# Layer-0 experts of a two-layer transformer kernel: VectorE takes both halves of the router-weight multiply, GpSimd takes the rotary add of the next step

## The reference, cut to what matters

```python
xn = _layernorm(x, axis=-1)
x = x + _L0_attn_ref(xn, ...) + _L0_ffn_ref(xn, ...)

# in _L0_attn_ref: the same projection serves as queries and keys, and both are rotated
bq = bq * jnp.cos(qf) * qs + _rotate_half(bq) * jnp.sin(qf) * qs
bk = bk * jnp.cos(freqs) * inv_s + _rotate_half(bk) * jnp.sin(freqs) * inv_s
sim = jnp.einsum('bwie,bwje->bwij', bq, bk)
attn = jax.nn.softmax(sim, axis=-1)
out = jnp.einsum('bwij,bwje->bwie', attn, bv)
return out @ w_out.T

# in _L0_ffn_ref: one shared expert and eight routed ones, weighted per token (top 2)
h1 = jax.nn.gelu(jnp.einsum('td,edh->teh', flat, rw1) + rb1[None], approximate=False)
expert_out = jnp.einsum('teh,ehd->ted', h1, rw2) + rb2[None]
mixed = jnp.einsum('ted,te->td', expert_out, weights)
return (shared_out + mixed)
```

## Time and profile before

| what | value |
|---|---|
| median of 3 runs | 1160.11 us (1159.56 to 1161.54) |
| the profiled execution's own time | 1158.52 us |
| its span in the trace | 1157.2 us |
| mean granted clock of TensorE | 0.964 of full speed |
| busy: PE, DVE, ACT, POOL | 90%, 62%, 45%, 40% of the span |
| stages `experts0` of steps 2 to 6 in the trace | about 40 us each, one every 133 us |

### The profile page before, as it was taken

One profiled execution on the slowest core, in us unless ns is written; L12 is line 12 of the kernel. 1 busy time (PEld: TensorE's weight loads), 2 busy tenths in 40 slices (PEclk: granted clock), 3 DMA queues, 4 the chain that ended last, 5 costly groups with the idle time before them and its releaser, 6 DMA issues.

```text
span 1157.2 us, 13293 instructions
## 1 busy us (share of the span) xinstructions
PE 1045.4 (90%) x4472; PEld 634.5 (55%) x4472; DVE 713.7 (62%) x1485; ACT 519.4 (45%) x1209; POOL 457.7 (40%) x337
## 2 busy tenths in 40 slices
PE   4877856899999998999999998999989999989998
PEld 2543434546655565656655565655655466655655
DVE  4845525564884758574884848665784848712743
ACT  3442453326264443735255453645356363634322
POOL 4229310274215642084413742075411852043434
PEclk9898877989999999999999999999999999989999
DMA  6041000322023220233004220232104220232151
GB/s 239 1 138 37 9 1 1 113 73 72 11 73 87 64 55 10 90 78 82 18 14 128 64 73 0 84 80 78 37 10 122 64 73 1 83 76 73 37 119 47
DMA packets 34581, 72.77 MB, mean 63 GB/s; under 512 B 4553, under 2 KB 5330, under 8 KB 34130
## 3 DMA queue, kind: packets, MB, share of 16 engines
q1 hardware_dynamic: 33074, 68.59, 21.0%
q10 hardware_dynamic: 1440, 3.35, 0.8%
HBM read 69.04 MB, written 2.88 MB: 62 GB/s over the span
## 4 chain that ended last, share of the span: by engine, by line
PE 65%; DVE 9%; issue 7%; POOL 4%; ACT 2%; DMA 0%; DVEq 0%; POOLq 0%; ACTq 0%
PE ps L689 9%; PE ps L577 7%; PE ps L440 6%; PE ps L441 6%; PE ps L442 6%; PE ps L512 5%; PE ps L488 4%; PE ps L500 4%; PE ps L664 3%; POOL pw L1742 2%; PE ps L585 2%; PE ps L635 2%; PE ps L471 2%; PE ps L653 1%; PE ps L643 1%
## 5 line engine op out<-in xcount | busy, mean ns | idle before, releaser
L1742 POOL TENSOR_TENSOR pw<-pw,wb 128x512 f32<-128x512 f32 x64 | 94.9, 1483 | 215.7 <-ACT pw L1002 190.8
L577 PE MATMUL ps<-pw,w_w 128*128 128x512 f32 x288 | 146.3, 618 | 24.0 <-POOL pw L1742 24.0
L1078 ACT ACTIVATE wide<-ps 128x512 f32<-128x512 f32 x136 | 80.9, 595 | 177.3 <-PE ps L442 176.5
L1749 POOL TENSOR_TENSOR atc<-atc,wide 128x512 f32<-128x512 f32 x64 | 82.4, 1289 | 168.1 <-DVE atc L1470 168.1
L1002 ACT ACTIVATE pw<-ps,w_cols 128x512 f32<-128x512 f32 x144 | 99.0, 687 | 107.8 <-PE ps L442 104.6
L1355 DVE TENSOR_TENSOR pw<-pw,wb 128x512 f32<-128x512 f32 x64 | 62.3, 974 | 128.5 <-ACT pw L1002 121.5
L961 ACT ACTIVATE pw<-ps,nmax 128x256 f32<-128x256 f32 x256 | 117.2, 473 | 25.7 <-DVE nmax L1291 25.6
L1291 DVE TENSOR_REDUCE nmax<-ps 128x4 f32<-128x1024 f32 x64 | 78.2, 1224 | 58.7 <-PE ps L488 58.2
L512 PE MATMUL ps<-pt,vr 128*64 128x256 f32 x512 | 74.7, 416 | 27.6 <-DVE pt L1300 27.5
L1300 DVE COPY pt<-ps 128x512 f32<-128x512 f32 x128 | 82.3, 685 | 23.7 <-PE ps L500 23.6
L577 PEld LDWEIGHTS ps<-pw,w_w 128*128 128x128 f32 x288 | 51.8, 193 | 79.4 <-POOL pw L1742 47.2
(11 more groups left out here) (219 smaller groups left out, 2188.4 us busy)
## 6 DMA issues: line engine op xcount, KB each, us to landing
wb<-scratch SPq DMA_DIRECT2D x128, 256.0 KB, 4.0
wb<-scratch SPq DMA_DIRECT2D x32, 512.0 KB, 5.5
wide<-scratch SPq DMA_DIRECT2D x16, 512.0 KB, 6.1
xin<-in_x SPq DMA_DIRECT2D x8, 256.0 KB, 2.7
out<-wide SPq DMA_DIRECT2D x8, 256.0 KB, 2.1
w_w<-in_w ACTq DMA_DIRECT2D x1, 1152.0 KB, 11.0
wb<-in_w SPq DMA_DIRECT2D x1, 1152.0 KB, 11.2
w_ed<-in_ed ACTq DMA_DIRECT2D x1, 1024.0 KB, 15.8
```

The costliest lines, as they stand in the source:

```text
L577: pe.matmul(bank(ACC), w2[:, e, c, :], hid[:, n % 4, :], start=n == 0, stop=n == 2 * E0 + 1).then_inc(*DOWN0.one)
L1742: pool.tensor_tensor(hid[:, n % 4, :], hid[:, n % 4, :], wb[:, e, :], ALU.mult).then_inc(*HID_POOL.one)
L1749: pool.tensor_tensor(hh[h], hh[h], sgl[:, (c + 1) % 3, :], ALU.mult).then_inc(*HH_POOL.one)
```

## The change

DVE's `hidden` now multiplies both halves of each expert, and POOL's is gone. POOL's `rope_add` takes the place of DVE's in the stages `experts0` (those that DVE does for step 0, ahead of and in `attention(0)`, stay). POOL's stage is written anew: per pair of heads it is `normalise`, `rope_turn`, `rope_add`; in step 0 it is two `split_staged`, `rope_turn`, `rope_add`, and the four `normalise` come at the end. The two events of `hidden` become one, `HID`, with 16 counts per step.

```diff
@@ events
-        HID_DVE, HID_POOL = event("hid_dve", E0), event("hid_pool", E0)
+        HID = event("hid", 2 * E0)
@@ SP, weights_layer0 (and in the same way weights_layer1)
-                        w.wait_ge(*HID_DVE.at(0, 2 * k + 1))
-                        w.wait_ge(*HID_POOL.at(0, 2 * k + 1))
+                        w.wait_ge(*HID.at(0, 4 * k + 3))
@@ PE, down0
-                        w.wait_ge(*(HID_POOL if c else HID_DVE).at(s, e))
+                        w.wait_ge(*HID.at(s, 2 * e + c))
@@ DVE
             def hidden(s, e):
-                n = 2 * place0(e)
-                w.wait_ge(*GELU.at(s, n))
-                w.wait_ge(*wb_layer0(e // 2, s))
-                dve.tensor_tensor(hid[:, n % 4, :], hid[:, n % 4, :], wb[:, e, :],
-                                  ALU.mult).then_inc(*HID_DVE.one)
+                for n in range(2 * place0(e), 2 * place0(e) + 2):
+                    w.wait_ge(*GELU.at(s, n))
+                    w.wait_ge(*wb_layer0(e // 2, s))
+                    dve.tensor_tensor(hid[:, n % 4, :], hid[:, n % 4, :], wb[:, e, :],
+                                      ALU.mult).then_inc(*HID.one)
@@ DVE, experts0
                 hidden(s, 4)
                 if more:
-                    rope_add(n, 0)
                     rope_in(n, 2, 2)
                 if first:
                     split_staged(5)
                 hidden(s, 5)
                 if more:
-                    rope_add(n, 1)
                     rope_in(n, 3, 6)
                 if first:
                     split_staged(6)
                 hidden(s, 6)
-                if more:
-                    rope_add(n, 2)
                 if first:
                     split_staged(7)
                 hidden(s, 7)
                 if first:
                     split_staged(8)
-                if more:
-                    rope_add(n, 3)
@@ POOL
-            def hidden(s, e):
-                n = 2 * place0(e) + 1
-                w.wait_ge(*GELU.at(s, n))
-                w.wait_ge(*wb_layer0(e // 2, s))
-                pool.tensor_tensor(hid[:, n % 4, :], hid[:, n % 4, :], wb[:, e, :],
-                                   ALU.mult).then_inc(*HID_POOL.one)
+            def rope_add(s, p):
+                h = p % 2
+                w.wait_ge(*STRAIGHT.at(s, p))
+                w.wait_ge(*TURNED_Q.at(s, p))
+                pool.tensor_tensor(kr[:, p, :], kr[:, p, :], rtmp[:, h, :], ALU.add)
+                pool.tensor_tensor(qr[:, p, :], qr[:, p, :], qka[:, h, :], ALU.add).then_inc(*ROPED.one)
@@ POOL, experts0
-                if first:
-                    split_staged(0)
-                for e in range(E0):
-                    hidden(s, e)
-                    if first:
-                        split_staged(e + 1)
-                    if more and e in (2, 3, 5, 6):
-                        rope_turn(n, (0, 0, 0, 1, 0, 2, 3)[e])
-                    if e in (1, 4):
-                        normalise(s, 2 * (e // 4))
-                        normalise(s, 2 * (e // 4) + 1)
+                for p in range(PAIRS):
+                    if first:
+                        split_staged(2 * p)
+                        split_staged(2 * p + 1)
+                    else:
+                        normalise(s, p)
+                    if more:
+                        rope_turn(n, p)
+                        rope_add(n, p)
+                if first:
+                    for p in range(PAIRS):
+                        normalise(s, p)
+                    split_staged(8)
```

More of the change, by code:

```diff
@@ L366, in weights_layer1 @@
                 elif s < LAST:
-                    w.wait_ge(*HID_DVE.at(s + 1, 2 * k + 1))
-                    w.wait_ge(*HID_POOL.at(s + 1, 2 * k + 1))
+                    w.wait_ge(*HID.at(s + 1, 4 * k + 3))
                 else:
@@ L1788, in experts0 @@
             def experts0(s):
-                x, n, first, more = s - 1, s + 1, s == 0, s < LAST
-                if first:
-                    split_staged(0)
-                for e in range(E0):
-                    hidden(s, e)
-                    if first:
-                        split_staged(e + 1)
-                    if more and e in (2, 3, 5, 6):
-                        rope_turn(n, (0, 0, 0, 1, 0, 2, 3)[e])
-                    if e in (1, 4):
-                        normalise(s, 2 * (e // 4))
-                        normalise(s, 2 * (e // 4) + 1)
+                n, first, more = s + 1, s == 0, s < LAST
+                for p in range(PAIRS):
[7 more added lines that the diff above has]
+                        rope_add(n, p)
+                if first:
+                    for p in range(PAIRS):
+                        normalise(s, p)
+                    split_staged(8)
             def experts1(s):
```

## The result

The changed kernel takes 1169.81 us (median of 7 runs, 1166.74 to 1172.98), against 1160.11 before (median of 7): the ratio is 1.0095, with a 95% interval of 1.007 to 1.012. One of the seven runs before took 2009.1 us, and the ratio leaves it out. The changed kernel is slower, by some 10 us where 15 were predicted. The profiled execution took 1167.9 us, its span is 1166.6 us, and the mean granted clock 0.968.

What follows compares the result with a forecast made beforehand. PE, busy 90% of the span, was taken as the bound. Middle steps +18.5, step 1 +2.1, step 0 +1.8 and step 7 -6.6 gave +15.8 us; forecast 1175.5, own range 1168 to 1183, wider range 1160 to 1186.

Steps and rivals of the forecast that it cites:

- The clock in the middle steps: Steps 2 to 6, first products of `attention_out`: PE's clock falls behind the 2.9 us wait, costing 2.1 us a step.
- step 1: PE gains 7 us through the experts, then waits for the last `normalise`: nothing gained, 2.1 us lost to the slow clock.
- step 0: All `normalise` come last on POOL, ending at 116.9 against 117.22: less 0.3, plus 2.1 for the clock, 1.8 us.
- POOL's chain: Middle steps, first `normalise` to end of last: 16 instructions, ten collisions with DVE and three waits, 24.8 us (24.2 to 25.6).
- The middle steps without the clock: Steps 2 to 6: PE waits 2.9 us for the last `normalise`, so `attention_out` starts 1.6 us later than before.
- the rival in which the clock holds: Middle steps: the clock does not fall behind the wait at `attention_out`, so +5.3 us, 1165; chance 0.14.
- I find each one landed before POOL comes to it: First step: SP's loads of split weights run later but land before POOL needs them, so no wait was counted.
- Step 7: No rotation there, and `hidden` no longer waits for POOL's `normalise`: 12.84 us become 2 x 3.11, a gain of 6.6.
- DVE costed at nothing: DVE swaps 8 adds for 8 halves of `hidden` a step; these are ready in time, with 1 us cover: no cost.
- Dearer collisions: Each collision holds the other engine off for its whole instruction, 1.94 us a pair instead of 1.68: 1193 us; chance 0.07.
- Quick POOL: Collisions are rarer and POOL's 16 instructions take 21.9 us, so PE never waits: 1145 us, or 1154 at 23.2; chance 0.12.
- Swallowed: Short waits of PE in the next stage absorb the delay at `attention_out`: about 1160 us, within 0.2%; chance 0.07.

Runs made afterwards that it cites:

- Experiment 1: Changed kernel with POOL's third and fourth `normalise` both ahead of the turn of pair 2 in steps 1 to 7: 1146.01 us, ratio 0.9895 to the kernel before.
- experiment 8: Changed kernel with DVE's `hidden` multiplications of experts 3 to 7 cut to 8 of 512 columns in steps 2 to 6: 1148.71 us, ratio 0.9906.
- experiment 4: Kernel before the change, engines as they were, with its two pairs of `normalise` behind experts 3 and 5 instead of 1 and 4: 1135.39 us, ratio 0.9802.
- Experiment 9: Kernel before with DVE multiplying both `hidden` halves and keeping the adds; POOL turns pairs 0 and 1, does all `normalise`, turns 2 and 3: 1149.63 us.

## Why the prediction was right, and where its sizes were off

The mechanism came as described: the last `normalise` in 16th place, `attention_out` waiting for it, a clock that can fall behind that wait. Experiment 1 takes the place away and the loss goes; experiment 8 leaves the place, shortens the chain and the wait goes too. The time lies in the range and in the forecast's own range of 1168 to 1183, 5.7 us below the number. Between the two traces the sum came to +9.4 us instead of +15.8. The clock in the middle steps makes 5.4 of this difference. The misses of step 1 (1.6 too high) and of step 0 (1.5 too low) cancel, which is luck. Term by term:

- **POOL's chain.** Predicted 24.8 us, measured 24.4 to 24.5. The sum of 16 starts and ten collisions held. The wait of an add for the turn ahead of it showed as well: 639.72 to 641.13 is 1.41 us between starts instead of 1.23, so 0.18 where I took 0.1.
- **The middle steps without the clock.** Predicted: PE waits 2.9 us and loses 1.6 a step. Measured: it waits 2.62 to 2.68 and loses, with 1.7 taken off where the clock fell, 1.3 to 1.7: 7.4 us over five steps, predicted 8.0.
- **The clock in the middle steps** is the term that was mis-sized: "I expect it to fall here too", 2.1 us in each of five, 10.5 together. It fell in three, at 1.7 us each: 5.1. The forecast and the rival in which the clock holds were both true, each in some steps, and a clock of 1.00 behind `attention_out`, named as a sign of being wrong, was there in two. The runs of the changed kernel point the same way: the four at a mean clock of 0.965 to 0.968 took 1166.74 to 1169.81 us, the three at 0.958 to 0.962 took 1171.85 to 1172.98. But the slowest lie 5.1 us above the profiled one, and two more falls would give 3.4, so the middle steps alone don't explain the spread.
- **Step 1.** Predicted +2.1, measured +0.5. The last `normalise` sets the end there, as I had it: POOL is done at 254.65 and PE starts at 254.70. Set back by the 3.3 us that step 0 lost, that is 251.4, while I had 253.6 (today's 253.62). I took the chain of the middle steps, 24.8 us; here it is 231.31 to 254.65 = 23.3, as DVE itself waited for POOL twice (2.50 and 2.47 us ahead of its shuffles) and only 8 of its halves fell beside the chain. The denominators also came 0.9 us earlier by that count (228.84). Against these 2.3 us stand the slow products, 6.35 us instead of 3.60: 2.75.
- **Step 0.** Predicted +1.8, measured +3.3. The last `normalise` ended at 118.4, not 116.9, and the slow products behind it cost 2.6 us (6.16 instead of 3.60), not 2.1. The step that failed is "I find each one landed before POOL comes to it". SP loads a piece only behind POOL's low part of the last but one. One such load was issued at 85.08, behind that low part, and DVE waited for it 3.51 us (until 88.03). For the next load the low part was ready at 86.27, but SP's order has the denominators ahead of it. It was issued at 89.11, behind the two loads of `wide`, and took 6.8 us where the others took 2.9 or 3.0. For this one DVE waited 1.72 us, and POOL 2.92 for DVE's cast. SP, its load in the DMA view (last figure: us to landing), DVE and POOL:

```profile
87.74 1.32 SPq L386 DMA_DIRECT2D wide<-scratch  x2
89.11 0.60 SPq L338 DMA_DIRECT2D gu<-in_eu  x1
```

```profile
gu<-in_eu SPq DMA_DIRECT2D x1, 256.0 KB, 6.8
```

```profile
95.92 0.43 DVE L1475 CAST eu<-gu 128x512 fp32r<-128x512 f32 x1 [1.72 <-DMA gu<-in_eu]
```

```profile
96.43 1.66 POOL L1756 TENSOR_TENSOR eu<-gu,eu 128x512 fp32r<-128x512 f32 x1 [2.92 <-DVE eu L1475]
...
113.44 4.92 POOL L1728 TENSOR_TENSOR atc<-atc,wide 128x512 f32<-128x512 f32 x4
```

- **Step 7.** Predicted -6.6, measured -6.6.
- **DVE costed at nothing.** In the middle steps that held: no down product waited for it. The wait of 5.2 us in all is in steps 0 and 1, where PE then waited for the last `normalise` all the same.
- **What was not read.** Of the 24.0 us, the prediction names the waits of steps 1, 4 and 7 and one of 2.42 in step 0. The longest, 10.12 us in step 0 (experiment 4), is not among them. Its forecast for step 0 didn't need it, as it goes from POOL's own chain.
- **The rivals.** *Dearer collisions* (0.68 + 1.26 us for a pair) falls: POOL's chain took 24.4 to 24.5 us. By the Trainium skill, "SBUF — State Buffer", section "SBUF: two separate sides", a VectorE instruction with two SBUF inputs and a GpSimd one that reads SBUF exclude each other: the first to start has the shared ports for its whole instruction, and the other blocks fully. Experiment 8 puts the price for POOL at 0.41 us for each of DVE's multiplications, less than the 0.68 us that DVE's takes alone; no run here shows blocking for the whole 0.68. By the prediction's own 1.94 and 1.68 us, ten collisions would have cost 2.6 us more, not 2.4. *Quick POOL*, with the wait gone below 21.9 us, is what experiment 8 made on purpose at 20.4 us. *Swallowed* falls: the delay is there at the start of every next stage.

Still open is why the clock fell behind three of five waits that differ by no more than 0.06 us. Experiment 9 shows the same with shorter ones: of five waits of 2.29 to 2.31 us, two were followed by a fall. No experiment was made on it.

## What to carry to other kernels

Read the queue of a helper engine by its due dates, not by its load: POOL was busy 38% of the time, and the place of one instruction in its queue was worth 24 us. When work is swapped between two engines, count the places by which each instruction that another engine waits for is moved, and then try the orders. Try the order on the old kernel as well, since here four fifths of the gain lay there. And parts of a change can't be judged alone: one gave -4 us, the other +43, and both with the right order -30.

## What the runs showed of the hardware

- Multiplications and adds of 128x512 floats by DVE and POOL, with all operands in SBUF, slow each other: DVE's took 1.75 us instead of 0.68, and each cost POOL 0.41 (experiment 8). A DVE multiplication that reads a PSUM bank beside a busy POOL stays at 0.67 us:

```profile
643.79 0.66 DVE L1273 TENSOR_TENSOR rtmp<-ps,w_rope 128x512 f32<-128x512 f32 x1
```

- A POOL instruction that waits for the result of the one just ahead of it starts 1.41 us behind that one's start, instead of 1.23.
- Nearly the same idle time of PE, 2.62 to 2.68 us, was followed by a granted clock of 0.50 to 0.55 in three steps, and of 1.00 in two (windows above for one of each). So one profile doesn't fix this cost. The seven runs of the changed kernel spread over 6 us, the slower ones at the lower mean clock.
